# Building the dense edge matrices of a graph network by pairs of edge tiles instead of triples

## The reference

```python
src = jax.random.randint(..., (200000,), 0, 6250)
dst = (6250 * jax.random.uniform(..., (200000,)) ** 2.0).astype(jnp.int32)   # then sorted
...
deg = segment_sum(ones, dst)
norm = jnp.clip(deg, 1.0) ** (-0.5)
h = segment_sum((x * norm[:, None])[src], dst) * norm[:, None]   # layer 0, three times; layer 3, once
...
msg = edge_weight[:, None] * h[cols]                             # layer 2, twice
h = segment_sum(msg, rows, num_segments=n)
```

## Time and profile before

| | us |
|---|---|
| median of 3 runs | 9939.35 (9939.27 to 9943.32) |
| the profiled execution | 9935.04 |
| its span, first to last instruction | 9933.2 |
| setup, up to the first DVE operation of the build | 134.0 |
| build, up to the last DVE operation of it | 134.0 to 4072.1 |
| wait for the last stores, flags and degrees | 4072.1 to 4176.1 |
| the rest: counts passes, MLP, hyperbolic layers, last layer | 4176.1 to 9933.2 |

### The profile page before, as it was taken

How to read it: one execution, slowest core, us unless ns; L and a number is a source line. 1 busy time by engine, 2 the same in 40 slices (tenths; PEclk the granted TensorE clock), 3 DMA queues, 4 the chain that set the end, 5 groups by cost and what they waited for, 6 DMA issues and landing times. The chain is left out here.

```text
span 9933.2 us, 193226 instructions
## 1 busy us (share of the span) xinstructions
PE 7507.0 (76%) x59876; PEld 5740.8 (58%) x59877; DVE 4212.0 (42%) x16253; ACT 2509.1 (25%) x14806; POOL 1929.9 (19%) x3544
## 2 busy tenths in 40 slices
PE   4988876555555555499885999999997993696285
PEld 3877765444444444388753888888884442343173
DVE  7988876544544544501122222222224006203714
ACT  0244445444544454200000111111111002001101
POOL 1111110000000000000001777777772000000000
PEclk9999998877877777699975777777776996897586
DMA  0011111111111111277732222222221990694062
GB/s 23 22 62 52 68 69 68 59 69 69 58 69 69 69 58 69 83 277 276 255 114 59 48 48 48 48 48 48 48 48 37 305 297 24 210 298 145 7 240 83
DMA packets 283195, 1005.48 MB, mean 101 GB/s; under 512 B 84845, under 2 KB 85997, under 8 KB 253613
## 3 DMA queue, kind: packets, MB, share of 16 engines
q1 hardware_dynamic: 232814, 952.06, 28.0%
q0 software_dynamic: 50176, 51.48, 2.8%
HBM read 749.76 MB, written 243.85 MB: 100 GB/s over the span
## 5 line engine op out<-in xcount | busy, mean ns | idle before, releaser
L1410 PEld LDWEIGHTS banks<-T 128*128 128x128 bf16 x31752 | 2237.8, 117 | 329.7 <-issue 90.2
L1410 PE MATMUL banks<-T 128*128 128x128 bf16 x31752 | 2386.7, 229 | 0.0
L1407 PE MATMUL banks<-T 128*128 128x512 bf16 x2646 | 1087.5, 411 | 1284.2 <-ACT ACC L1168 565.1
L547 POOL DMA_INDIRECT WORK<-table,idx x1568 | 1498.8, 956 | 596.5 <-issue 441.5
L743 DVE TENSOR_SCALAR T<-T 128x128 bf16<-128x128 bf16 x7956 | 1519.5, 247 | 0.0
L739 DVE TENSOR_SCALAR T<-T 128x128 bf16<-128x128 f16 x2652 | 661.3, 249 | 1460.7 <-PE banks L1410 1436.2
L1379 PE MATMUL banks<-T,WORK 128*128 128x250 bf16 x4900 | 1061.6, 272 | 64.2 <-DVE WORK L826 64.2
L1442 PE MATMUL banks<-T,WORK 128*64 128x392 f32 x3200 | 1062.8, 495 | 18.0 <-DMA T<-dense_w 11.0
L1380 PE MATMUL banks<-T,WORK 128*128 128x250 bf16 x4900 | 1061.3, 269 | 0.0
L1407 PEld LDWEIGHTS banks<-T 128*128 128x128 bf16 x2646 | 271.5, 103 | 1359.1 <-issue 812.7
L740 DVE TENSOR_SCALAR T<-T 128x512 bf16<-128x512 f16 x2652 | 918.5, 346 | 0.0
(11 more groups left out here) (277 smaller groups left out, 6339.9 us busy)
## 6 DMA issues: line engine op xcount, KB each, us to landing
T<-dense_w SPq DMA_DIRECT2D x400, 784.0 KB, 4.2
T<-dense_c SPq DMA_DIRECT2D x100, 1562.5 KB, 6.9
dense_w<-WORK SPq DMA_DIRECT2D x128, 1220.0 KB
T<-dense_c SPq DMA_DIRECT2D x100, 1500.0 KB, 7.0
WORK<-in_eaT SPq DMA_DIRECT2D x196, 256.0 KB
dense_c<-T SPq DMA_DIRECT2D x13, 3062.5 KB, 10.3
dense_c<-ACC SPq DMA_DIRECT2D x12, 3062.5 KB, 9.2
WORK<-table,idx POOLq DMA_INDIRECT x1568
```

Of the source, the lines that this page charges most:

```text
L547: nc.gpsimd.indirect_dma_start(out=g_sb[:, u, c * D:(c + 1) * D], out_offset=None, in_=table, in_offset=bass.IndirectOffsetOnAxis(ap=idx[: ...
L1407: T.matmul(banks[:, 2 + u, :], planes[:, v, 0, :], hot[:, v, :], start=begins and v == 0, stop=False, skip_group_check=True)
L1410: last = T.matmul(banks[:, u, j * P:(j + 1) * P], keys[:, j, :], planes[:, v, 1 + k, :], start=begins and v == 0 and j == 0 and k == 0, st ...
```

## The change

- **Groups of 5 destinations** instead of 10: 1250 groups of 245 keys, 10 sets in the setup instead of 5.
- **Pairs** instead of triples. DVE makes for two tiles at once, with the two tiles interleaved element by element (index `t`), one comparison of 128x768 (two halves of the key and `low`, each of 128 values, for two tiles), and directly behind it one multiplication of 128x768 (the one-hot of low by the three parts of the weight). The lists, and all operands of both operations, are bf16. Both are TENSOR_TENSOR with an operand repeated by a step of zero.
- **Two slots** (`SLOTS = 2`) of a pair each, instead of three of a tile. One semaphore `pair_ready` and one `pair_free` count pairs.
- **An odd number of pairs for each group** (`bitwise_or` with 1), so that a group's first pair lies always in the slot of its number, and PE has its addresses as constants. With pair u of a group begun in slot v, PE's inner loop does two pairs a turn.
- **PE** does for a tile one matmul of 245 columns and six of 128 (two of them 129; the 129th column holds ones and sums the weights' one-hots to the degrees). Counts are written to PSUM in the order h, d while they are read in the order d, h, so neighbouring columns of this matmul land five fp32 words apart. All of a group lies in one bank, and four banks turn (`TURN = 4`).
- **ACT** copies a group with two copies (258 and 245 columns), and the degrees of five groups with one copy of 10 columns.
- **SP** stores five groups with three DMAs (112, 10 and 1 partitions, pieces of 1 KB) and does not wait for their landing; ACT waits for it when it comes to the same half of the buffer again. SP also stores zeros once for the rows behind the last node.
- **Register loads** of several values at once: PE one for four groups, ACT one for five, POOL two for five.
- **Degrees**: PE sums with selecting matrices in 13 steps of up to 500 nodes.

```diff
-GROUP = 10
+GROUP = 5
-QUAD = 3
+QUAD = 2
+SLOTS = 2
+TURN = 4
...
-                sp.dma_start(batch[:, 0:full * 4, :].rearrange("b (m j) l -> m b (j l)", j=4), dense_out[0:full, u, :, :]).then_inc(batch_stored, 16)
...
-                sp.wait_ge(batch_stored, n * 32 + 32)
-                sp.sem_inc(batches_free, 1)
+                most, pairs = P // 16 * 14, KEYS // 2
+                for first, past in ((0, most), (most, pairs)):
+                    sp.dma_start(batch[:, 2 * first:2 * past, :].rearrange("b (m j) l -> m b (j l)", j=2),
+                                 dense_out[first:past, slot, :, 1:1 + 2 * P]).then_inc(batch_stored[slot], 16)
+                sp.dma_start(batch[:, 2 * pairs:KEYS, :].rearrange("b k l -> k b l"),
+                             dense_out[pairs:pairs + 1, slot, :, 1:1 + P]).then_inc(batch_stored[slot], 16)
...
+                fin(V.tensor_scalar(g_int, g_int, 1, None, ALU.bitwise_or))
...
+                def hots(now, s):
+                    v = s % SLOTS
+                    dve.wait_ge(quad_taken, now)
+                    dve.wait_ge(pair_free, now)
+                    V.tensor_tensor(planes[:, v, 0:HOTS].rearrange("p (k n t) -> p k n t", k=3, t=QUAD),
+                                    iota2.unsqueeze(1).to_broadcast([P, 3, P, QUAD]),
+                                    quads[:, s, 0:3, :].unsqueeze(2).to_broadcast([P, 3, P, QUAD]), ALU.is_equal).then_inc(hots_ready, 1)
+
+                def weights(now, s):
+                    v = s % SLOTS
+                    dve.wait_ge(hots_ready, now)
+                    V.tensor_tensor(planes[:, v, HOTS:PLANES].rearrange("p (k n t) -> p k n t", k=3, t=QUAD)[:, :, 0:P, :],
+                                    planes[:, v, 2 * P * QUAD:3 * P * QUAD].rearrange("p (n t) -> p n t", t=QUAD).unsqueeze(1).to_broadcast([P, 3, P, QUAD]),
+                                    quads[:, s, 3:6, :].unsqueeze(2).to_broadcast([P, 3, P, QUAD]), ALU.mult).then_inc(pair_ready, 1)
+
...
+                def pair(now, v, u, begins):
+                    pe.wait_ge(pair_ready, now)
...
+                    for t in range(QUAD):
+                        T.matmul(banks[:, u, 0:KEYS].rearrange("p (h d) -> p d h", h=HI), lows[:, t, :], hot[:, t, 0:KEYS].rearrange("p (d h) -> p d h", h=HI),
+                                 start=begins and t == 0, stop=False, skip_group_check=True)
...
+                    last.then_inc(pair_free, 1)
```

More of the change, by code:

```diff
@@ L128, in gnn_kernel @@
         roundf = WORK[0:1, 5603:5604]
[L130 to L135, removed]
@@ L318, in load, with loads, bounds_of, deltas_of @@
             return nc.s_assert_within(eng.value_load(of), low, high, skip_runtime_bounds_check_because="it was worked out within them")
-        def quads_of(eng, g, n):
-            bounds = ((0, GROUPS * COLS), (1, GROUPS * COLS), (-QUAD * GROUPS * COLS, COLS))
-            return [load(eng, ranges_sb[0:1, ds(g * 4 + k, 1)], bounds[k][0], bounds[k][1]) for k in range(n)]
+        def loads(eng, of, low, high):
+            _, values = nc.values_load_multi_w_load_instructions(of, engines=[eng.engine], min_val=low, max_val=high,
+                                                                 skip_runtime_bounds_check_because="they were worked out within them")
+            return values
+        def bounds_of(eng, g, n):
+            return loads(eng, ranges_sb[0:1, 0, ds(g, n + 1)], 0, GROUPS * COLS)
+        def deltas_of(eng, g, n):
+            return loads(eng, ranges_sb[0:1, 2, ds(g, n)], -QUAD * GROUPS * COLS, COLS)
         def column_of(eng, q, delta):
-            return nc.s_assert_within(eng.snap(q * QUAD + delta), 0, COLS - 1, skip_runtime_bounds_check_because="the ranges were made so")
+            return nc.s_assert_within(eng.snap(q * QUAD + delta), 0, KCOLS - QUAD, skip_runtime_bounds_check_because="the ranges were made so")
         def before(eng, p, R):
@@ new lines, in groups @@
+                def groups(g0, n):
+                    bounds = bounds_of(pe, g0, n)
+                    for u in range(n):
+                        v, begin, past = u % SLOTS, bounds[u], bounds[u + 1]
+                        pe.wait_ge(group_copied, g0 + (u + 1))
+                        pair(begin + (1 + QRING), v, u, True)
+                        with pe.If(past > begin + 1):
+                            with pe.Fori(begin + 1, past, 2) as q:
+                                pair(q + (1 + QRING), 1 - v, u, False)
+                                pair(q + (2 + QRING), v, u, False)
@@ L1433, in build_dense @@
+                with pe.Fori(0, GROUPS // TURN) as i:
+                    groups(i * TURN, TURN)
+                groups(GROUPS // TURN * TURN, GROUPS % TURN)
+                pe.drain().then_inc(pair_free, QRING - SLOTS)
                 end()
@@ L1519, in _ @@
             R = load(pe, rounds_i[0:1, 0:1], 1, P)
-            pe.wait_ge(flag_step, at_flag(0, "all_ones"))
-            for i in range(BLOCKS):
-                for c in HALVES:
-                    begin(pe, at_deg, i, c)
-                    did(times(A2[c], all_ones, lambda j: NORM_full[:, i * BLK + c * PUB + j * SUB:i * BLK + c * PUB + (j + 1) * SUB]), c)
+            for i in range(DEG_STEPS):
+                if i >= 8:
+                    pe.wait_ge(deg_plus, i - 7)
+                groups = deg_nodes(i) // GROUP
+                to = banks[0:D, i % 8, 0:deg_nodes(i)].rearrange("p (g i) -> p i g", i=GROUP)
+                for n in range(GROUP):
+                    for j in range(2):
+                        last = T.matmul(to[:, n, :], sel[:, n, j, :], degp[:, i * DEG_GROUPS:i * DEG_GROUPS + groups, j],
+                                        start=n == 0 and j == 0, stop=n == GROUP - 1 and j == 1, skip_group_check=True)
+                last.then_inc(deg_summed, 1)
             end()
```

316 lines of the change are left out of this document (162 added, 154 removed).

## The result

The changed kernel takes 8801.7 us (median of four runs, 8797.2 to 8804.9) against 9941.3 for the kernel before (9939.3 to 9943.9): a ratio of 0.8853, interval 0.8838 to 0.8869, 11.5% faster. I had forecast 8264 and a range up to 8740.

The account below looks back on a forecast made before the run. The weights' store on two DMA engines was taken as the bound for most of the build, DVE in the crowded first groups. Forecast: 189 + 2242 (1808·1.24) + 16 + 54 + 5757 = 8258 us span, 8264 against the median; range 8010 to 8740.

Parts of the forecast that it names:

- Setup: Before the build: five more sets add 51 us and other work 4, so the build's first DVE operation comes at 189.
- count of pairs: In the build: 1808 pairs with the rounding to odd, 1592 without, each costing one period.
- everything behind the build: After the last DVE operation: 16 us to the flags, 54 for the degrees, then 5757 unchanged.
- The store at nothing: SP's weights' store in the build: under 5 us per five groups, covered by slack, so counted as no time.
- The rival that ended on the slower side: Weights' store stays on two engines at 80 ns a piece: 25 us a batch, about 12,270 us; chance 0.03.
- PE's part of a pair: PE in the build: a pair costs what a tile did before, 0.85 us, and 1.18 until the slot is back.
- The hand-over loop: DVE and PE in the build: filling, handing over and using two slots bounds it, 2.39 us for two pairs, 1.19 each.
- my rival of four times a column: PE's spread counts write costs four times a column: +0.61 us a pair, period 1.50, 8734 us; chance 0.10.
- POOL hidden: POOL in the build: a take every 0.44 us, loads and loop some 0.8 us a group, so no time added.
- The rival "POOL becomes the bound": POOL and DVE block each other reading SBUF: 1.3 to 1.5 us a pair, 8370 to 8730 us; chance 0.20.
- ACT hidden: ACT in the build: two copies a group, each under 437 ns, together under 0.87 us, so no time added.
- The clock: PE in the build runs at 2.4 GHz; the rival, a lower level, needs 1.7 us a pair, 9096 us; chance 0.04.

Follow-up runs that it names:

- four_ahead: Changed kernel with PE reading constant ones and DVE allowed four pairs ahead instead of two (results not the graph's): build 2680 us against 2787.
- span4: Changed kernel with POOL's register loads for four groups, aligned, instead of five: 0.8718 of the kernel before, build 2576 us.

## Why the prediction was wrong

- **Setup, count of pairs, DVE, everything behind the build: right.** 189 us and 189.7; 1808; 0.56 us an operation; 16 us to the flags and 14.1; 54 and 54.5; 5757 and 5756. The Trainium skill (VectorE: DVE Perf Modes, "The perf-mode tier table") gives tensor_tensor in bf16 twice the rate of fp32; the trace agrees: 559 ns are the 0.16 and half of the 0.80 us that 768 fp32 elements would take by the earlier trace rows.
- **The store at nothing: right for the wait, not for what else it touches.** ACT has no wait for a store among its longest, and the DMA share in the sparse part is 0.34 at 110 GB/s, where the earlier trace rows had 0.17 at 66. The rival that ended on the slower side is out. (Its 15.7 us a batch is where it would be as slow as the kernel before; the store would be the bound from 9.0, 7.23 pairs of 1.24.) But the stores go with longer register loads of POOL. The sum for the sparse part, estimated from the means, is 5.0 us for five takes, 0.54 between takes and loads, and 2 · 1.58 for the loads: 1.74 a pair, as measured. With the 1.13 us of the crowded part it would be 1.56. That is some 160 us from 1000 to 2900 (405 loads, 0.40 each), an estimate that no run with the stores left out has tested.
- **PE's part of a pair: the step that failed in the crowded part.** I took 0.85 us for two tiles from the earlier trace rows, by the number of columns. Measured are 1.15. Of the 0.30 too much, 0.17 are the spread write (twice 0.085; I had taken 0.10 a pair as its middle, with 0.20 as the upper bound, so it was inside the bounds and near their end), 0.04 the stride; the remaining 0.09 I didn't take apart. The time from PE's first weight load until DVE has the slot back grew with it from 1.18 to 1.43 us; on the period that is 0.12 to 0.15, where I had put 0.05. The Trainium skill (PSUM — Partial Sum Buffer, "Specifications") warns that a non-contiguous pattern slows matmuls significantly; the trace agrees, 373 against 280 ns for this one, though my rival of four times a column was too much.
- **The hand-over loop: right as a mechanism.** four_ahead takes it away and the crowded part drops to 1.17 to 1.21, where PE's own 1.15 for two tiles stands.
- **POOL hidden: the step that failed in the sparse part, and it cost most.** Two numbers of "a take every 0.44 us, and a register load of 0.29 twice for five groups" were wrong. The two COPY rows at 134.60 and 135.04 stood at the end of a wait: POOL's sequencer had prepared them ahead, and the engine drained its queue. A take costs the sequencer 0.95 to 1.0 us. The trace of the kernel before held that number already, 7 us earlier, where the sequencer ran ahead unhindered: its wait instruction stands three times between 127.2 and 129.3 us (the row is below), 1.05 us apart. And the loads of the earlier trace rows fetch one value; those of six and five values cost 1.39 and 1.17 us. In the sparse part, with one pair in nearly every group, five groups need 5.0 and 3.1 us by the medians, 1.62 a pair before any stall of DVE or PE; 1.74 is what came, which is the sum with the longer loads above.

```profile
L521 POOLq EVENT_SEMAPHORE  x3: 17/17/17, 127.2 to 129.3; - x3
```

- **The rival "POOL becomes the bound", with 0.20, was the right engine for the wrong reason.** I had argued the shared reading of SBUF. Signs of it are there in the crowded part, where POOL's COPY has a median of 316 ns next to 190 in the sparse one, while DVE stays at 559. The Trainium skill (SBUF — State Buffer, "Who interferes with whom") says that a DVE instruction with two SBUF inputs contends with a GpSimd one that reads SBUF; the longer COPY agrees with it. But in the sparse part, where POOL is the bound, its operations are short and its sequencer long. Its 1.3 to 1.5 us a pair was again under the 1.74, and so the range ended 62 us too low.
- **ACT hidden: right,** with 0.84 us for its two copies, though the one of the counts takes 0.45 where I had put each under 0.44.
- **The clock:** 1.00 in the crowded part, as taken. In the sparse one 0.94, which means the lower level for 12% of the time: it goes with PE's pauses, since span4, which touches POOL alone, brings it to 0.98.

## What to carry to other kernels

Take the price of an engine's step from a stretch in which that engine is late, never from rows that follow a wait: those show how fast a queue drains. When a change makes steps shorter and more frequent, add up every register, branch and load instruction of each sequencer per step, beside the busy times, because a page's busy share leaves them out. Take a sequencer's load not from a quiet stretch only, but with the DMA traffic that the new kernel will have beside it. And when a cause is doubled or halved, count in the trace that it was, before believing a zero.

## What the runs showed of the hardware

- **Register loads of several values depend on where they start.** In the changed kernel POOL's spans begin at multiples of five words. In order of time its bounds' loads (six values) take 1.39, 1.39, 1.39, 0.78 us and so on, the deltas' (five) 1.17, 1.17, 1.17, 0.57: every fourth, which begins at a multiple of four words, is short. ACT's six values take 2.64 and 0.76 in the same rhythm. Aligned: four values 0.32, five 0.57 on POOL, 0.54 on ACT and 0.58 on PE. ACT's split load doesn't fit this rule (three values from any start 0.70, the next three always 2.0), so the rule is not complete; why ACT pays more than POOL stays open. The rest would fit a load that fetches four values at a time where it begins at a multiple of four, and one at a time elsewhere: one piece takes 0.29 to 0.32 us, two 0.57 (five or eight values), three 0.78 to 0.81 (six or nine), five 1.17 and six 1.39. That is a reading of these figures which no run tested.
- **Register loads beside DMA traffic are longer:** in the changed kernel PE's loads take 0.59 us when the DMA engines are idle at their start and 1.17 when they are over 20% busy, POOL's 1.20 and 2.15 (means, 1000 to 2900 us). In the kernel before, the few of POOL's loads (16) that meet such traffic take 0.84 us instead of 0.29.
- **A PSUM write with 20 bytes between words** makes a matmul of 245 columns take 373 ns instead of 280 and costs 0.085 us a tile, while ACT reads such a pattern out of PSUM in the same 0.45 us as the other.
- **PE's granted clock fell around a pause.** It was 1.00 from 2506 to 2508, 0.52 and 0.63 in the next two stretches of 2 us, and 1.00 again from 2512. PE was busy for 0.72 of the 2 us before it fell and idle for the 1.66 up to 2508.38; the tile behind that (2508.38 to 2509.41) took 1.03 us instead of 0.57.

```profile
2508.38 0.59 PE L1460 MATMUL banks<-T 128*128 128x245 bf16 x1 [1.66 <-DVE T L792]
...
2509.41 0.61 PE L1460 MATMUL banks<-T 128*128 128x245 bf16 x1
```
